# Expert layer: routing weights spread over partitions by a store and broadcast loads instead of a product on TensorE

## The reference, cut to what matters

```python
scores = sigmoid(xf @ router_w.T)            # [2048, 64]
# groups of 8 experts, the best 4 groups, then the best 8 experts of those
w = take_along_axis(scores, topk_idx, 1)
w = w / (w.sum(-1, keepdims=True) + 1e-20)
g = ragged_dot(sorted_x, gate_w, ...)        # 64 experts, [128, 64] each
u = ragged_dot(sorted_x, up_w, ...)
h = silu(g) * u
o = ragged_dot(h, down_w, ...) * w           # added to the shared expert's output
```

## Time and profile before

| | us |
|---|---|
| median of 3 runs | 2452.66 (2448.4 to 2453.31) |
| profiled execution | 2450.8 |
| its span, first to last instruction | 2449.0 |
| PE busy | 2203.9 (90%) |
| DVE busy | 1652.6 (67%) |
| ACT busy | 1365.0 (56%) |
| POOL busy | 187.2 (8%) |
| first gate product of the experts starts | 1979.28 |
| last down product of the experts ends | 2339.39 |

### The profile page before, as it was taken

The page is one execution under the profiler, slowest core; times in us unless marked ns, Lnnn a source line. Parts: engine busy times, 40 slices in busy tenths (PEclk is TensorE's granted clock), DMA queues, the critical chain, the costliest instruction groups (busy, mean ns, idle before and its releaser), DMA issues. The chain is left out here.

```text
span 2449.0 us, 42836 instructions
## 1 busy us (share of the span) xinstructions
PE 2203.9 (90%) x16992; PEld 1014.7 (41%) x16992; DVE 1652.6 (67%) x2062; ACT 1365.0 (56%) x2663; POOL 187.2 (8%) x373
## 2 busy tenths in 40 slices
PE   5899999999988499999799999999998979999977
PEld 2233333323333122223356666666665434444443
DVE  6999999999923799997445555555554454444443
ACT  3788888888854288888444444444454312222233
POOL 3000000000001500000000000000000200000000
PEclk7899999999998699999999999999999989999988
DMA  4000000000000200000000000000000000000000
GB/s 137 11 14 7 8 14 14 11 7 12 1 1 26 90 16 27 20 10 2 11 13 5 1 4 4 5 1 4 1 1 1 23 10 16 19 16 19 16 9 26
DMA packets 42661, 39.19 MB, mean 16 GB/s; under 512 B 9509, under 2 KB 34085, under 8 KB 42352
## 3 DMA queue, kind: packets, MB, share of 16 engines
q1 hardware_dynamic: 40324, 34.56, 4.6%
q0 software_dynamic: 1488, 1.04, 0.2%
q10 hardware_dynamic: 668, 1.04, 0.1%
HBM read 29.85 MB, written 7.36 MB: 15 GB/s over the span
## 5 line engine op out<-in xcount | busy, mean ns | idle before, releaser
L853 ACT ACTIVATE a0p<-ps 128x512 f32<-128x512 f32 x1024 | 542.1, 599 | 113.4 <-PE ps L757 99.0
L863 DVE TENSOR_REDUCE a0nm<-ps 128x2 f32<-128x1024 f32 x512 | 588.0, 1216 | 12.3 <-PE ps L737 10.1
L771 PE MATMUL ps<-a0p,a0vst 128*32 128x256 f32 x4096 | 328.8, 393 | 25.7 <-ACT a0p L853 14.2
L853 ACT ACTIVATE a1p<-ps 128x512 f32<-128x512 f32 x512 | 274.6, 596 | 76.8 <-PE ps L757 68.8
L863 DVE TENSOR_REDUCE a1nm<-ps 128x2 f32<-128x1024 f32 x256 | 295.2, 1217 | 15.0 <-PE ps L737 14.1
L757 PE MATMUL ps<-a0qm,a0k 32*128 32x512 bf16 x1024 | 274.0, 387 | 0.1
L1521 DVE TENSOR_REDUCE canm<-ps 128x1 f32<-128x128 f32 (+7 forms) x256 | 182.1, 753 | 115.1 <-PE ps L1358 114.5
L1737 ACT ACTIVATE ex_s<-ps 128x512 f32<-128x512 f32 x128 | 76.4, 597 | 280.8 <-PE ps L1692 280.8
L737 PE MATMUL ps<-a0k,a0q 32*128 32x512 bf16 x1024 | 204.0, 397 | 28.5 <-DVE a0nm L863 21.8
L1465 ACT ACTIVATE cap_long<-ps,canm 128x1024 f32<-128x1024 f32 (+3 forms) x128 | 121.4, 952 | 174.7 <-DVE canm L1521 174.7
L1835 DVE TENSOR_TENSOR ex_su<-ex_s,ps 128x512 f32<-128x512 f32 x128 | 88.0, 688 | 183.7 <-PE ps L1695 183.7
(11 more groups left out here) (315 smaller groups left out, 2785.6 us busy)
## 6 DMA issues: line engine op xcount, KB each, us to landing
a0parts<-a0parts_sb SPq DMA_DIRECT2D x8, 384.0 KB, 3.6
a1parts<-a1parts_sb SPq DMA_DIRECT2D x8, 384.0 KB, 3.5
ex_wg<-in_ex_gate SPq DMA_DIRECT2D x32, 64.0 KB, 1.8
ex_wu<-in_ex_up SPq DMA_DIRECT2D x32, 64.0 KB, 1.9
ex_wd<-in_ex_down SPq DMA_DIRECT2D x32, 64.0 KB, 1.8
mod_w<-in_L_wmod SPq DMA_DIRECT2D x4, 384.0 KB, 6.3
a0q<-a0parts SPq DMA_DIRECT2D x62, 24.0 KB
a1q<-a1parts SPq DMA_DIRECT2D x30, 48.0 KB
```

The costliest lines, as they stand in the source:

```text
L771: last = pe.matmul(R.ps[32 * j:32 * j + 32, 6, cols], vst[:, g, s, j * HG // 4, :], p[:, s % 2, j, cols], start=(g == 0 and s == 0 and hal ...
L853: act.activation(p[:, s % 2, e, :], R.ps[:, score_bank(n), :], ACT.Exp).then_inc(exp_done, 1)
L863: dve.tensor_reduce(nm[:, u % 2, tb, 2 - 2 * z:4 - 2 * z, hf], R.ps[:, bank:bank + 2, :], X_AXIS, ALU.max, negate=True).then_inc(bank_free, 1)
```

## The change

The three bf16 parts, `choose`, `wsplit` and the spreading product go. The fp32 weights are transposed as they are (16 transposes, [128, 64] to [64, 128]), copied by ScalarE and VectorE in turn into `wT` [64 experts, 2048 tokens], stored by SP in two halves into a DRAM tensor `w_dram` and loaded back, each expert's row repeated over 64 partitions, into `wb` [128, 2 slots, 2048] in fp32. The first pair's load is cut in four (expert by half of the tokens); every other pair's is one DMA of 1 MB, `load_routed`, issued on SP's queue, in the loop behind the three weight loads of the pair. `hid` is `su` times `wb`. Gate and up have two PSUM banks each (4 and 6, 5 and 7), `hid` four buffers, and the down product runs two steps behind instead of one.

```diff
--- before.py
+++ after.py
@@ -1572,7 +1572,9 @@
 
     sb = lambda n, s, d=F32: ctx.enter_context(nc.sbuf_tensor("ex_" + n, s, d))
     sem = lambda n: nc.alloc_semaphore("ex_" + n)
-    wsplit = sb("wsplit", [128, 2, N], BF16)
+    w_dram = nc.dram_tensor("ex_w_dram", [E, N], F32, kind="Internal").ap()
+    wT = sb("wT", [E, N])
+    wb = sb("wb", [128, 2, N])
     rw, bias, before, shw = W.rw, W.bias, W.before, W.shw
     score = sb("score", [128, TB, E])
     sbias = sb("sbias", [128, TB, E])
@@ -1586,9 +1588,9 @@
     left = sb("left", [128, TB, E])
     top = sb("top", [128, TB, 8])
     tot = sb("tot", [128, TB])
-    parts = sb("parts", [128, TB, 2, 4, E // 2], BF16)
-    prod, scored, routed, top_step, parted, turned, out = (
-        sem(n) for n in ("prod", "scored", "step", "top", "parted", "turned", "out"))
+    prod, scored, routed, top_step, weighed, turned, out_a, out_d = (
+        sem(n) for n in ("prod", "scored", "step", "top", "weighed", "turned", "out_a", "out_d"))
+    w_stored = [sem("w_stored0"), sem("w_stored1")]
 
     shs, shu, shh = sb("shs", [C, 2, CW]), sb("shu", [C, 2, CW]), sb("shh", [C, 2, CW])
     sh_g, sh_u, sh_silu, sh_copied, sh_hid, sh_down = (
@@ -1598,15 +1600,15 @@
     wg = sb("wg", [C, 2, C])
     wu = sb("wu", [C, 2, C])
     wd = sb("wd", [C, 2, C])
-    choose = sb("choose", [128, EP // 2, C], BF16)
     s = sb("s", [C, 2, CW])
     su = sb("su", [C, 2, CW])
-    hid = sb("hid", [C, 2, CW])
-    const_loaded = sem("const")
+    hid = sb("hid", [C, 4, CW])
     ld = [sem("ld0"), sem("ld1")]
-    g_full, silu_done, u_full, su_done, w_full, hid_done, d_done, res_done = (
-        sem(n) for n in ("g_full", "silu", "u_full", "su", "w_full", "hid", "d", "res"))
-    G_BANK, U_BANK, W_BANK = 4, 5, 6
+    w_ld = [sem("w_ld0"), sem("w_ld1")]
+    w_first = [sem("w_first0"), sem("w_first1")]
+    g_full, silu_done, u_full, su_done, hid_done, d_done, res_done = (
+        sem(n) for n in ("g_full", "silu", "u_full", "su", "hid", "d", "res"))
+    G_BANK, U_BANK = 4, 5
     STEPS = EP // 2
 
     def on_sp(sp):
@@ -1615,16 +1617,29 @@
             sp.dma_start(wu[:, slot, :], dram["ex_up"][bass.ds(pair * C, C), :]).then_inc(ld[slot], 16)
             sp.dma_start(wd[:, slot, :], dram["ex_down"][bass.ds(pair * C, C), :]).then_inc(ld[slot], 16)
 
+        def load_routed(pair, slot):
+            sp.dma_start(wb[:, slot, :], w_dram[bass.ds(pair * 2, 2), :].unsqueeze(1).broadcast_to([2, EH, N]))\
+              .then_inc(w_ld[slot], 16)
+
         load(0, 0)
         load(1, 1)
+        for b in range(B):
+            sp.wait_ge(out_a, b + 1)
+            sp.wait_ge(out_d, b + 1)
+            sp.dma_start(w_dram[:, b * T:(b + 1) * T], wT[:, b * T:(b + 1) * T]).then_inc(w_stored[b], 16)
+        for b in range(B):
+            sp.wait_ge(w_stored[b], 16)
+            for e in range(2):
+                sp.dma_start(wb[e * EH:(e + 1) * EH, 0, b * T:(b + 1) * T],
+                             w_dram[e:e + 1, b * T:(b + 1) * T].broadcast_to([EH, T])).then_inc(w_first[b], 16)
+        load_routed(1, 1)
         with sp.Fori(1, STEPS) as kk:
             for slot in range(2):
                 sp.wait_ge(d_done, kk * 8 + (4 * slot - 4))
                 load(kk * 2 + slot, slot)
+                load_routed(kk * 2 + slot, slot)
 
     def on_pool(pool):
-        pool.memset(parts[:, :, :, 3, :], 0.0).then_inc(parted, 1)
-        pool.dma_start(choose[:], dram["choose"]).then_inc(const_loaded, 16)
         for i in range(SH):
             pool.wait_ge(sh_silu, i + 1)
             pool.wait_ge(sh_copied, i + 1)
@@ -1665,11 +1680,9 @@
 
         pe.wait_ge(sh_silu, SH)
         pe.wait_ge(sh_copied, SH)
-        pe.wait_ge(parted, 6)
+        pe.wait_ge(weighed, 1)
         for tb in range(TB):
-            for i in range(2):
-                dst = R.ps[:, 4 + tb // 4, :].bitcast(BF16)[:, ((tb % 4) * 2 + i) * 128:((tb % 4) * 2 + i + 1) * 128]
-                last = pe.transpose(dst, parts[:, tb, i].rearrange("p a e -> p (a e)"), R.identb[:])
+            last = pe.transpose(R.ps[0:E, 4 + tb // 4, (tb % 4) * 128:(tb % 4 + 1) * 128], score[:, tb, :], R.ident[:])
             if tb % 4 == 3:
                 last.then_inc(turned, 1)
 
@@ -1677,38 +1690,35 @@
 
             m = kk * 8 + i
             pe.wait_ge(hid_done, m + 1)
-            pe.matmul(R.ps[:, i % 4, :], wd[:, (i // 4) % 2, :], hid[:, i % 2, :], start=False,
+            pe.matmul(R.ps[:, i % 4, :], wd[:, (i // 4) % 2, :], hid[:, i % 4, :], start=False,
                       stop=True, skip_group_check=True).then_inc(d_done, 1)
 
-        def step(kk, half, first=False):
+        def step(kk, first=False):
 
             for i in range(8):
                 m = kk * 8 + i
                 slot, c = i // 4, i % 4
                 if c == 0:
                     pe.wait_ge(ld[slot], kk * 48 + 48)
-                if not (first and i == 0):
-                    pe.wait_ge(silu_done, m)
-                pe.matmul(R.ps[:, G_BANK, :], wg[:, slot, :], h_chunk(R, c), start=True, stop=True).then_inc(g_full, 1)
-                if not (first and i == 0):
-                    pe.wait_ge(su_done, m)
-                pe.matmul(R.ps[:, U_BANK, :], wu[:, slot, :], h_chunk(R, c), start=True, stop=True).then_inc(u_full, 1)
-                if not (first and i == 0):
-                    pe.wait_ge(hid_done, m)
-
-                pair = choose[:, bass.ds(kk * 2 + (slot - half * (EP // 2)), 1), :]
-                pe.matmul(R.ps[:, W_BANK, :], pair, wsplit[:, half, c * CW:(c + 1) * CW],
-                          start=True, stop=True).then_inc(w_full, 1)
-                if not (first and i == 0):
-                    down(kk, i - 1)
-
-        pe.wait_ge(out, TB // 4)
-        pe.wait_ge(const_loaded, 16)
-        step(0, 0, True)
-        with pe.Fori(1, STEPS // 2) as kk:
-            step(kk, 0)
-        with pe.Fori(STEPS // 2, STEPS) as kk:
-            step(kk, 1)
+                if not (first and i < 2):
+                    pe.wait_ge(silu_done, m - 1)
+                pe.matmul(R.ps[:, G_BANK + 2 * (i % 2), :], wg[:, slot, :], h_chunk(R, c), start=True, stop=True)\
+                    .then_inc(g_full, 1)
+                if not (first and i < 2):
+                    pe.wait_ge(su_done, m - 1)
+                pe.matmul(R.ps[:, U_BANK + 2 * (i % 2), :], wu[:, slot, :], h_chunk(R, c), start=True, stop=True)\
+                    .then_inc(u_full, 1)
+                if first and i >= 2:
+                    down(0, i - 2)
+                if not first:
+                    down(kk if i >= 2 else kk - 1, i - 2 if i >= 2 else i + 6)
+
+        pe.wait_ge(out_a, 2)
+        pe.wait_ge(out_d, 2)
+        step(0, True)
+        with pe.Fori(1, STEPS) as kk:
+            step(kk)
+        down(STEPS - 1, 6)
         down(STEPS - 1, 7)
 
     def on_act(act):
@@ -1722,11 +1732,9 @@
             act.activation(shs[:, i % 2, :], R.ps[:, G_BANK, :], ACT.Silu).then_inc(sh_silu, 1)
             act.wait_ge(sh_u, i + 1)
             act.activation(shu[:, i % 2, :], R.ps[:, U_BANK, :], ACT.Copy).then_inc(sh_copied, 1)
-        for g in range(TB // 4):
+        for g in (0, 2):
             act.wait_ge(turned, g + 1)
-            src = R.ps[:, 4 + g, :].bitcast(BF16).rearrange("p (t i c) -> p i t c", t=4, i=2)
-            act.activation(wsplit[:, :, g * CW:(g + 1) * CW].rearrange("p i (t c) -> p i t c", t=4), src, ACT.Copy)\
-               .then_inc(out, 1)
+            act.activation(wT[:, g * CW:(g + 1) * CW], R.ps[0:E, 4 + g, :], ACT.Copy).then_inc(out_a, 1)
 
         def step(kk, first=False):
             for i in range(8):
@@ -1734,7 +1742,7 @@
                 act.wait_ge(g_full, m + 1)
                 if not (first and i < 2):
                     act.wait_ge(su_done, m - 1)
-                act.activation(s[:, i % 2, :], R.ps[:, G_BANK, :], ACT.Silu).then_inc(silu_done, 1)
+                act.activation(s[:, i % 2, :], R.ps[:, G_BANK + 2 * (i % 2), :], ACT.Silu).then_inc(silu_done, 1)
 
         step(0, True)
         with act.Fori(1, STEPS) as kk:
@@ -1812,31 +1820,29 @@
         dve.wait_ge(routed, n)
         after(dve.reciprocal(tot[:], tot[:]))
         dve.wait_ge(routed, n)
-        tt(score[:], score[:], tot[:].unsqueeze(2).broadcast_to([128, TB, E]), ALU.mult)
-        dve.wait_ge(routed, n)
-
-        part = lambda i: parts[:, :, :, i, :]
-        h = lambda x: x[:].rearrange("p t (i e) -> p t i e", i=2)
-        for i, op in enumerate(((part(0), h(score)), (h(masked), h(score), part(0)), (part(1), h(masked)),
-                                (h(left), h(masked), part(1)), (part(2), h(left)))):
-            if len(op) == 2:
-                dve.tensor_copy(*op).then_inc(parted, 1)
-            else:
-                dve.tensor_tensor(*op, ALU.subtract).then_inc(parted, 1)
-            dve.wait_ge(parted, i + 2)
+        dve.tensor_tensor(score[:], score[:], tot[:].unsqueeze(2).broadcast_to([128, TB, E]), ALU.mult).then_inc(weighed, 1)
```

(23 more changed lines are left out.)

## The result

| | before | after |
|---|---|---|
| median, us | 2451.98 (2448.4 to 2453.31) | 2728.11 (2727.55 to 2729.69) |
| ratio | | 1.113, 95% interval 1.111 to 1.1149 |
| span of the profiled execution | 2449.0 | 2726.4 |

The change makes the kernel 276 us slower, where 2749 (2712 to 2818) was predicted. From the page of the kernel after: span and PE's busy time, two groups of instructions (busy us, mean ns, then idle time ahead of them with its releaser), and four DMA issues.

A forecast was written before the change was run, and what follows sets the result against it. TensorE bound the kernel before; after, the DMA queue would, at 20.9 us a pair against 10.3. First transfer lands at 2000.2, thirty more at 20.9, tail 9: +296.8 us on 2450.8 is 2747.6, plus 1.9 to the median: 2749 (2712 to 2818).

The forecast's parts named there:

- Two engines: In the loop, each 1 MB `load_routed` runs on two DMA engines, the outermost count of its source, 64 rows each.
- 0.315 us a row: Price of an 8 KB row on one engine in the 1 MB loads; 64 rows make 20.2 us a transfer.
- First transfer at 2000.2: Ahead of the loop, the load for pair 1 is issued at 1978.4 and lands at 2000.2.
- Tail 9 us: After the last transfer, `hid` and six products take 9 us, between 5.8 at full clock and 11 at half.
- Weights in time: In the loop, weights queued behind a megabyte land 0.7 + 1.6 us after it, needed only after 4.1 us.
- The queue stays full: In the loop, the next transfer is queued after 19.3 us at most, under the 20.9 of a pair.
- 28.2 us of product: In the expert loop, dropping the spreading product takes 128 steps by 0.22 us = 28.2 us off TensorE.
- `choose` worth nothing: Ahead of the loop, removing GpSimd's DMA of `choose` gains nothing, as it was done long before the transposes.
- Rival A: The loop's 1 MB loads spread over all 16 engines, TensorE stays the bound, 33.5 us off, 2419; chance 0.09.
- threshold, four engines: In the loop, Rival A decides from four engines on: 10.8 us a pair, under the 11.16 of the kernel before.
- Rival B: The loop's rows cost more than in a stream: 0.47 us each, 30.1 us a transfer, 3056; chance 0.08.
- Rival C: In the loop TensorE stays at half clock, 20.6 us a pair; moves only the tail, by 2 us; no separate chance.

The follow-up runs named there:

- e1: The changed kernel with each pair's 1 MB load cut into two DMAs, one expert each, source [64, 2048], on 16 engines: 2410.58 us, ratio 0.9835.
- e7: The changed kernel with each pair's load as two DMAs, one expert each, source [2, 32, 2048], on two engines: 2736.93 us, ratio 1.1167.
- e4: The kernel before without the spreading product, routing weights left out of the result: 2423.02 us, ratio 0.9887.
- e12: The changed kernel with each pair's load as four DMAs of 32 partitions, source [4, 8, 2048], on four engines: 2502.18 us, ratio 1.0205.
- e11: The changed kernel with a 16-engine load of one row repeated 128 times, second expert getting the first's weights: 2413.52 us, ratio 0.9847.
- e10: The changed kernel with weights stored twice and a 16-engine load of 128 different rows, wrong weights on experts: 2417.49 us, ratio 0.9863.
- e9: As e1, but each DMA reads 64 different rows instead of one row 64 times, wrong weights on experts: 2411.74 us, ratio 0.984.

## Why the prediction was right

- **Two engines** was read from the small packets of the earlier trace rows and is what the trace shows: 2 a transfer. e1 and e7, alike but for the outermost count (64 and 2), show that this alone turns 2411 into 2737; the changed kernel has 2728. The outermost 2 is a step over two experts in the changed kernel and a repetition in e7; both run on two engines (260 small packets in e7's view of 2100 to 2200, 5 x 48 + 5 x 4).
- **0.315 us a row** was the term that was mis-sized. It was 0.306: in the trace's packet records the rows of a stream start at that distance and overlap a little (each takes 0.309), so 64 of them take 19.6 us and a pair 20.33, not 20.9. Over the transfers that is 17 of the 21 us by which the forecast was too high. The lower bound of the earlier trace rows, 0.301, was nearer.
- **First transfer at 2000.2**: 1998.83, but this near only by luck. The copies ended at 1970.65 and not at 1974.4, 3.7 us early; from there to the issue of the load took 5.4 us, not 4.0, and from the issue to `hid` 22.8, not 21.8.
- **Tail 9 us**: 2608.66 to 2617.70, 9.0. **Weights in time**: gate never waited. **The queue stays full**: it does, with 6 us to spare.
- **28.2 us of product**: 28.8 by e4, hidden in the changed kernel, as TensorE is no longer the bound.
- **`choose` worth nothing** was wrong by 4.4 us (the first gate product came at 1970.75, not near 1974.5): I asked when it was done and not what it delayed.
- **Rival A** was right as a mechanism and priced 8 us too high (2419 against 2411). `choose` is 4.4 of them; 2.8 more lie in code that the change doesn't touch (first and last row of the table of the two spans), where chance alone can do as much (single runs of the kernel before lie between 2448.4 and 2453.31). Its threshold, four engines, was wrong: e12 has four engines at the full rate and is slower than before. Comparing a transfer with a pair's time left out the way from landing to the next issue.
- **Rival B** did not occur: a row took 0.31 us. Two engines on one DRAM row (e7, 0.316) and 16 on one (e11, 0.36, against 0.38 for 128 rows in e10) cost nothing either.
- **Rival C**: the granted clock was at 0.50 for some 10 us a pair, of which PE worked some 5. The queue stayed the bound, so it moved the tail only.

## What to carry to other kernels

Look at the outermost count of a DMA's source before its bytes: a broadcast written [2, 64, n] is carried by two engines, and the count of small packets in the DMA view tells it in a kernel that already has such a load. Two loads of 64 partitions with the repetition outermost are enough, if 1 MB a pair at half the rate still fits; check it against the round of a buffer (landing, use, next issue), not against the compute time alone. A load that is done long before its use can still make somebody else late: `choose`, on GpSimd's queue, held back the weights on SP's.

## What was not expected of the hardware

- A 64-partition destination costs 0.56 to 0.57 us per 8 KB row on 16 engines, a 128-partition one 0.36 to 0.38 (e9, e1 against e10, e11), whatever the source.
- Repeating one DRAM row costs nothing: e11 (one row, 128 times) 0.36, e10 (128 rows) 0.38.
- Four engines: 0.40 us a row on average where they write 16 partitions apart (28% of the rows at 0.62), 0.32 where 8 apart. Two engines 32 partitions apart: 0.316, as they run six to seven rows out of step.
- Two of GpSimd's two-engine loads ran side by side (up to 110 GB/s), two of SP's one after the other (52 to 56).
